# A graph-attention block on one Trainium2 core: turning the normalised rows on VectorE and through memory instead of on TensorE

## What is computed

```python
nx = _ln(x, ln1_g, ln1_b)
q, k, v = nx @ wq + bq, nx @ wk + bk, nx @ wv + bv        # split into 8 heads of 32
bias = where(adj > 0, 0.1 * adj * adj, -inf)
attn = softmax(q @ k.T / sqrt(32) + bias)
x1 = x + (attn @ v) @ wo + bo
n2 = _ln(x1, ln2_g, ln2_b)
out = x1 + gelu(n2 @ w1 + b1) @ w2 + b2                    # w1: 256 -> 1024, w2: 1024 -> 256
```

## Time and profile before

| | |
|---|---|
| median of three runs | 1406.34 us |
| the profiled execution | 1403.53 us, its span 1401.6 us |
| PE matmul busy | 1357.0 us, 97% of the span |
| DVE busy | 1188.8 us, 85% |
| ACT busy | 1135.6 us, 81% |
| POOL busy | 558.4 us, 40% |
| 16 DMA engines | 39.8% busy, 129 GB/s |
| mean granted clock of TensorE | 0.987 of full speed |

### The profile page before, as it was taken

How to read it: one execution, slowest core, us unless ns; L and a number is a source line. 1 busy time by engine, 2 the same in 40 slices (tenths; PEclk the granted TensorE clock), 3 DMA queues, 4 the chain that set the end, 5 groups by cost and what they waited for, 6 DMA issues and landing times.

```text
span 1401.6 us, 34084 instructions
## 1 busy us (share of the span) xinstructions
PE 1357.0 (97%) x11612; PEld 1167.6 (83%) x11612; DVE 1188.8 (85%) x2002; ACT 1135.6 (81%) x3336; POOL 558.4 (40%) x553
## 2 busy tenths in 40 slices
PE   8679999999999999999999999999999999999997
PEld 7568888888888888888888888888888888888876
DVE  4888898888898888898888889888889888889862
ACT  3678889888888888888988888988888888888753
POOL 3353334544333454333545333454333345433320
PEclk8789999999999999999999999999999999999999
DMA  4434333444333444333444433343443344433330
GB/s 150 132 125 143 130 117 122 154 134 144 127 117 125 139 142 142 120 127 121 137 149 131 135 130 118 122 153 127 145 132 110 126 146 142 142 120 121 103 116 23
DMA packets 147257, 180.17 MB, mean 129 GB/s; under 512 B 13584, under 2 KB 130576, under 8 KB 147216
## 3 DMA queue, kind: packets, MB, share of 16 engines
q1 hardware_dynamic: 147216, 179.63, 39.8%
HBM read 95.69 MB, written 83.89 MB: 128 GB/s over the span
## 4 chain that ended last, share of the span: by engine, by line
PE 91%; ACT 5%; DVE 2%; issue 1%; POOL 0%; DMA 0%; SPq 0%; ACTq 0%; DVEq 0%; POOLq 0%
PE work L378 27%; PE work L380 25%; PE work L379 25%; PE area L436 6%; PE work L483 4%; PE work L457 4%; ACT qk_all L656 2%; ACT soft L613 1%; DVE soft L842 0%; ACT late_memory L680 0%; ACT late_memory L691 0%; PE work L385 0%; DMA wa_raw<-in_L_gnn_wq 0%; DVE wa_raw L854 0%; DVE soft L818 0%
## 5 line engine op out<-in xcount | busy, mean ns | idle before, releaser
L613 ACT ACTIVATE soft<-soft,nmax 128x128 f32<-128x128 f32 x1024 | 396.9, 395 | 4.7 <-DVE nmax L826 4.4
L1018 POOL TENSOR_TENSOR ve<-mv,eps 128x4 f32<-128x4 f32 x64 | 13.0, 203 | 771.9 <-DVE mv L891 664.6
L378 PE MATMUL work<-w_hi,hid_parts 128*128 128x256 f32 x1024 | 295.4, 288 | 1.4 <-ACT late_memory L691 1.1
L380 PE MATMUL work<-w_hi,hid_parts 128*128 128x256 f32 x1024 | 286.0, 279 | 0.0
L379 PE MATMUL work<-w_lo,hid_parts 128*128 128x256 f32 x1024 | 285.9, 279 | 0.0
L927 DVE TENSOR_TENSOR hid_parts<-late_memory,hid_parts 128x512 fp32r<-128x512 f32 x256 | 225.2, 882 | 21.8 <-ACT hid_parts L701 21.6
L691 ACT ACTIVATE late_memory<-work,b_col 128x512 f32<-128x512 f32 x256 | 171.9, 683 | 69.6 <-PE work L380 53.3
L378 PE MATMUL work<-nt_hi,w_hi 128*128 128x512 f32 x512 | 211.8, 414 | 3.9 <-DVE nt_lo L917 3.9
L378 PEld LDWEIGHTS work<-w_hi,hid_parts 128*128 128x128 f32 x1024 | 191.9, 187 | 12.0 <-DVE xt_lo L917 5.8
L379 PE MATMUL work<-nt_lo,w_hi 128*128 128x512 f32 x512 | 201.4, 393 | 0.0
L380 PE MATMUL work<-nt_hi,w_lo 128*128 128x512 f32 x512 | 200.5, 392 | 0.0
(11 more groups left out here) (95 smaller groups left out, 3075.7 us busy)
## 6 DMA issues: line engine op xcount, KB each, us to landing
moved_blocks<-wa_raw SPq DMA_DIRECT2D x128, 512.0 KB, 2.7
probt<-moved_blocks SPq DMA_DIRECT2D x512, 128.0 KB, 2.9
xin<-in_x SPq DMA_DIRECT2D x32, 512.0 KB, 3.9
out<-res SPq DMA_DIRECT2D x128, 128.0 KB, 2.1
adj_in<-in_adj SPq DMA_DIRECT2D x32, 256.0 KB, 2.9
res<-in_L_gnn_w SPq DMA_DIRECT2D x1, 1024.0 KB, 9.9
late_memory<-in_L_gnn_w SPq DMA_DIRECT2D x1, 1024.0 KB, 12.4
wa_raw<-in_L_gnn_wq SPq DMA_DIRECT2D x1, 256.0 KB, 3.9
```

What stands on the lines that cost most here:

```text
L378: pe.matmul(o, lhs_hi, rhs_hi, start=first, stop=False)
L380: return pe.matmul(o, lhs_lo, rhs_hi, start=False, stop=last)
L613: a = act.activation(soft[:, b % 2, h, :], soft[:, b % 2, h, :], ACT.Exp, bias=nmax[:, b % 2, h:h + 1], accum_out=rsum[:, b % 2, h:h + 1])
```

## The change

Both turns leave TensorE. VectorE transposes the normalised rows of a whole group in 32x32 blocks into a buffer (`flat_blocks`, one instruction of 128x1024 for each kind). One DMA sends that buffer to DRAM (`send_flat`) and four bring it back (`fetch_flat`) over the old normalised rows (`xraw` is `xhat`'s memory, `nraw` is `nhat`'s). ScalarE makes the high part from there (`flip_hi`), and `flip_lo` moves from VectorE to GpSimd. `ident`, its build and the 16 matmuls against it at the start are gone.

The x rows are prepared one step sooner (normalised for group `step + 2`), and the MLP is later: the first two `up` units of a group still run in step 2, at its end, the others and `down` in step 3 (`-3`). In the diff the second `flip_lo` and the last `body` are GpSimd's; the bodies of the other engines are left out, and their new order is shown further down in three pieces. The bodies of all engines are in a new order, and so is `UNITS`, from 30 units to 26. Another waiting rule is added to `stats1`, and the small bias products of the start move by one score.

```diff
-AWAKE = 16
-UNITS = [("mix", 0, -1, 3), ("nt", 0, -2, 0), ("nt", 1, -2, 1), ("qk", 2, 0, 2), ("qk", 3, 0, 0),
+UNITS = [("v", 1, 0, 0), ("mix", 2, -1, 3), ("up", 2, -3, 1), ("up", 3, -3, 2), ("proj", 2, -1, 3),
...
-FIRST, EARLY, LATE = -2, 4, 2
+FIRST, EARLY, LATE = -2, 6, 2
...
+        flat = {k: sb(f"{k}_flat", [P, RPB, GB * DC, HD]) for k in ("xt", "nt")}
...
+        nraw = late_memory[:, 0:GB * D]
+        xraw = xhat[:, :, :].rearrange("p b d -> p (b d)")
...
+            def send_flat(step, off, kind):
...
+                sp.wait_ge(flat_ready[kind], step.through(off, 1, 0))
+                sp.dma_start(moved_flat[kind].rearrange("i k j n -> (i k) (j n)"),
+                             flat[kind][:, :, :, :].rearrange("p j m t -> p (j m t)")).then_inc(flat_sent[kind], 16)
+
+            def fetch_flat(step, off, kind):
...
+                raw = xraw if kind == "xt" else nraw
+                sp.wait_ge(flat_sent[kind], step.through(off, 1, 0, 16))
+                for j in range(RPB):
+                    sp.dma_start(raw[j * HD:(j + 1) * HD, :].rearrange("p (i n) -> p i n", i=RPB),
+                                 moved_flat[kind][:, :, j, :].rearrange("i k n -> k i n")).then_inc(flat_landed[kind], 16)
...
-            pe.wait_ge(ident_ready, 1)
-            for _ in range(AWAKE):
-                pe.matmul(spare, ident[:, :], ident[:, :], start=True, stop=True)
...
-            def flip(step, off, kind, c):
...
-                src, ready = (xhat, xhat_ready) if kind == "xt" else (nhat, nhat_ready)
-                free(step, kind, c)
-                for b in range(GB):
-                    if c == 0:
-                        pe.wait_ge(ready, step.through(off, GB, b))
-                    mm = pe.transpose(work[:, bank_of(kind, c), b * P:(b + 1) * P],
-                                      src[:, b, c * P:(c + 1) * P], ident[:, :])
-                mm.then_inc(full[kind], 1)
...
             def flip_hi(step, off, kind, c):
...
-                act.wait_ge(full[kind], step.through(off, DC, c))
-                act.activation(dst[:, c, :], work[:, bank_of(kind, c), :], ACT.Copy)\
-                   .then_inc(hi_taken[kind], 1)
+                act.wait_ge(flat_landed[kind], step.through(off, 1, 0, LAND))
+                act.activation(dst[:, c, :].rearrange("p (b i t) -> p b i t", b=GB, i=RPB),
+                               raw.rearrange("p (i b c t) -> p b i c t", i=RPB, b=GB, c=DC)[:, :, :, c, :],
+                               ACT.Copy).then_inc(hi_taken[kind], 1)
...
             def norm1(step, off, b):
...
-                    need(act, full["xt"], step.through(off - 1, DC, DC - 1))
+                    need(act, taken["xt"], step.through(off - 1, DC, DC - 1))
...
             def stats1(step, off):
...
+                need(dve, x_rstd, step.through(off - 1, 1, 0))
...
-            def flip_lo(step, off, kind, c):
...
-                dve.tensor_tensor(lo[:, c, :], work[:, bank_of(kind, c), :], hi[:, c, :].bitcast(F32),
-                                  ALU.subtract).then_inc(taken[kind], 1)
+            def flat_blocks(step, off, kind):
...
+                src, ready = (xhat, xhat_ready) if kind == "xt" else (nhat, nhat_ready)
+                need(dve, flat_sent[kind], step.through(off - 1, 1, 0, 16))
+                if kind == "nt":
+                    need(dve, taken["nt"], step.through(off - 1, DC, DC - 1))
+                dve.wait_ge(ready, step.through(off, GB, GB - 1))
+                dve.transpose(flat[kind][:, :, :, :], src.rearrange("p b d -> p (b d)")
+                              .rearrange("p (m j k) -> p j m k", j=RPB, k=HD)).then_inc(flat_ready[kind], 1)
...
+            def flip_lo(step, off, kind, c):
...
+                pool.wait_ge(hi_taken[kind], step.through(off, DC, c))
+                pool.tensor_tensor(lo[:, c, :].rearrange("p (b i t) -> p b i t", b=GB, i=RPB),
+                                   raw.rearrange("p (i b c t) -> p b i c t", i=RPB, b=GB, c=DC)[:, :, :, c, :],
+                                   hi[:, c, :].bitcast(F32).rearrange("p (b i t) -> p b i t", b=GB, i=RPB),
+                                   ALU.subtract).then_inc(taken[kind], 1)
...
             def body(step):
-                rstd_of_x(step, 1)
                 result_start(step, -2)
+                residual_start(step, 0)
+                flip_lo(step, 1, "xt", 0)
+                flip_lo(step, 1, "xt", 1)
+                rstd_of_x(step, 2)
                 rstd_of_n(step, -1)
-                residual_start(step, 0)
-                edges(step, 1)
+                flip_lo(step, -2, "nt", 0)
+                flip_lo(step, -2, "nt", 1)
+                edges(step, 2)
```

## The result

The kernel after takes 1410.72 us (median of 18 runs, 1403.65 to 1415.22), the one before 1406.25 us in the same comparison. The ratio is 1.0038, with a 95% interval of 1.0025 to 1.0050: slower by 0.4%, where I had forecast 1371 us and a range of 1354 to 1402. The profiled execution after has a span of 1412.7 us.

The account below looks back on a forecast made before the run. TensorE's work was taken to bound the steady part. -59.5 (PE) + 9 (waits) + 15.5 (added step) + 5 (first group) - 5 (end) = -35, from 1406.3 to 1371 us, range 1354 to 1402.

Parts of the forecast that it names:

- PE, per step: TensorE's steady step: transposes and a wait go, 0.20 us returns; 1.86 us less, floor 39.78 us, -59.5 us over 32 groups.
- What must fit under the floor: Steady step: DVE 36.8, ACT 37.9, POOL 22.6 us fit under 39.78; waits 0.3 us a step, +9 us (0 to +54).
- GpSimd's subtractions hold VectorE: Rival, steady step: four new subtractions add 5.2 us to DVE, 42.0 us a step, 1426 us; 0.13 shared with late turn.
- The turn that is late in each step: Rival, steady step: PE waits for xt_lo or nt_lo; 2 us late gives 1420, 1 us 1391; 0.13 shared with GpSimd's holds.
- ScalarE as the bound: Rival, steady step: ACT's 37.9 us plus remaining waits bound it; 1409, or 1385 with half; no chance of its own.
- its first version: ScalarE rival with 3.5 us of its waits remaining: step 41.4 us, total +2.4, 1409 us.
- The page on table loads: ScalarE rival's support: 1380 ns drain per table switch; two new switches 5.3 us, ACT needs 40.6 a step, 1385 us.
- The two ends: Filling and emptying the pipeline: added attention step +15.5 us, first group +5 us, end -5 us.
- The third step with attention alone: Start of pipeline: one more step of about 33 us with 17.5 us of PE work; +15.5 us idle.
- The end: Last group's turn, now covered by the MLP of group 30; -5 us (-8 to 0).
- The first group: Start: longer way to PE's first projection, +7.3 us, part made up behind it; +5 us taken (0 to +13).

Follow-up runs that it names:

- the kernel with 24 activations: 24 tiny unused activations added on ScalarE in written-out step 2, ahead of the loop, against the kernel after; 1388.65 us, ratio 0.9878 to the kernel before.
- the kernel with both repairs: Kernel after with all steps written out, late loads behind the first x return, small bias products one score later; 1368.96 us, ratio 0.9747 to the kernel before.

## Why the prediction was wrong

I go by its own steps. Written out, without the loop's stall, the kernel takes 1382 us, which lies in my range; with the start repaired as well it is 1369, about my forecast. The kernel as it is loses the gain to one thing that I never looked at, and to one that I sized too small.

**PE, per step: right.** The floor I had at 39.78 us, and a written-out step takes 39.88. Without the loop 28 groups take 1113.68 us and before 1161.90, 48.2 less, 1.72 each. My 1.86 less 0.3 is 1.56.

**What must fit under the floor: right in work, wrong in what it left out. This is the step that failed.** I took +9 us for all waits, "what PE had before for all causes". It is about +3 in written-out steps and 33 with the loop: 11 x 2.75 = 30 us more. My loads were right: ScalarE has 1049.38 / 28 = 37.5 us of work a step (37.9 in the text), the turns on VectorE take 1.24 and 1.22. But I added up busy times and followed waits on semaphores only; the jump back had no term in the sum, because in the kernel before it cost nothing, 0.24 us from the jump to the next instruction. In the kernel after ScalarE's code lies so that each of the 11 jumps is followed by a fetch and stops it for 3.9 to 4.6 us. I had counted instructions for their durations and never for their number and place: 8 more for the loop's body on ScalarE (280 from jump to jump and not 272), and some 265 more ahead of it. That ScalarE now has little room makes the stall dear, 2.25 us a time and not 0.56, but doesn't cause it.

The rows of the groups for the kernel after, which answer to the earlier trace rows:

```profile
L934 DVE TENSOR_TENSOR hid_parts<-late_memory,hid_parts 128x512 fp32r<-128x512 f32 x256 | 228.6, 921 | 27.4 <-ACT hid_parts L706 26.8
L1040 POOL TENSOR_TENSOR xt_lo<-xhat,xt_hi 128x512 fp32r<-128x512 f32 x64 | 117.4, 1847 | 56.1 <-ACT xt_hi L650 56.1
L1040 POOL TENSOR_TENSOR nt_lo<-late_memory,nt_hi 128x512 fp32r<-128x512 f32 x64 | 81.0, 1287 | 5.8 <-ACT nt_hi L650 5.8
L696 ACT ACT_TABLE_LOAD x59 | 75.7, 1283 | 6.0 <-PE work L404 5.0
L617 ACT ACT_TABLE_LOAD x58 | 74.4, 1283 | 1.1
L926 DVE STREAM_TRANSPOSE xt_flat<-xhat 128x1024 f32<-128x1024 f32 x32 | 39.6, 1237 | 0.8 <-ACT xhat L674 0.7
```

**The rivals.** GpSimd's subtractions hold VectorE: falls. `hidden_lo` has a mean of 921 ns against 882, 10 us in 256; one of the two pairs of new subtractions is held itself, the x rows at 1847 ns, the n rows at 1287 as I took them. The turn that is late in each step: falls, PE waits for `xt_lo` in the steady part nowhere, and its 24.4 us are three waits of the start. ScalarE as the bound: the nearest, since the time came out as its first version says (1409). But its reason, the order's waits that would stay, is not what happened. In the written-out kernel ScalarE still waits 2.3 us a step ((1113.68 - 1049.38) / 28) and the step is 39.88 all the same; what makes the long steps is the stall. The page on table loads (the Trainium skill, ScalarE: Activation LUTs, What ACT_TABLE_LOAD costs) with its further 1380 ns at each switch is not borne out: 117 loads with 7.1 us of idle time ahead of them all, and ScalarE's written-out step fits into 39.88 us, for which 40.6 would have been too much.

**The two ends.** The third step with attention alone takes 33.3 us, forecast 33. PE's idle time from the mix of group 0 to that of group 3 went from 14.1 to 35.9 us, +21.8 where I had +15.5: besides the added step, the low parts of the late weights fell under POOL's additions. VectorE and POOL of the kernel after:

```profile
84.52 5.28 DVE L786 SCALAR_TENSOR_TENSOR w_lo<-res,cols_in,w_hi 128x1024 fp32r<-128x1024 f32 x2 [1.07 <-ACT w_hi L609]
89.72 3.34 DVE L789 TENSOR_TENSOR w_lo<-late_memory,w_hi 128x2048 fp32r<-128x2048 f32 x1
```

```profile
85.39 3.33 POOL L1060 TENSOR_TENSOR x<-xin,bo_rows 128x1024 f32<-128x1024 f32 x1
88.91 5.26 POOL L1040 TENSOR_TENSOR xt_lo<-xhat,xt_hi 128x512 fp32r<-128x512 f32 x2 [0.19 <-ACT xt_hi L650]
```

The first pair took 2.48 us before; both engines are slowed here, and PE waits 11.3 us behind it. The end: PE's idle time fell from 9.8 to 2.9 us, -6.9 for my -5.

**The first group: the second term that was too small,** +5 us with a bound of 13, measured +19.6 to the mix of group 0. Of these 9.2 - 2.9 = 6.3 are the way out behind the loads, which I had seen as possible and not put into the sum. That the bias products move by one score stands in the description of the change, and I gave it no price. With both repaired the mark is at 54.41, +4.7. A part is chance: up to that mark the kernel with 24 activations has the same work as the kernel after and reached it at 63.87, with a clock of 0.86 and not 0.74 between first projection and mix; the kernel with both repairs had 0.84 there.

## What to carry to other kernels

A change that adds, removes or moves instructions can make a loop's jump back dear on one engine, though the order, the waits and the busy times are all right. It shows as idle time with no releaser at the loop's first instruction, as a late first instruction behind the jump, and as packets on the instruction queue in the middle of the loop, where the kernel without a stall has none. How much of it reaches the end depends on that engine's slack. Compare the steps inside a loop with those written out, one by one: a period of two in steps that should be equal can be the loop. Before a loop is made longer or shorter, count each engine's instructions in it and ahead of it, and write it out once to see what it costs.

## What was not expected of the hardware

- A loop's jump back cost ScalarE 2.5 to 3.2 us of idle time, or nothing, depending on where the code lay: moved by 24 instructions it vanished, moved by 8 it stayed, 4 instructions fewer a loop (8 fewer ahead) removed it, and 14 more ahead brought it back.
- With twice the code an iteration PE stalled twice (2.46 and 3.10 us), VectorE once (2.88): 7.9 us a jump ((1153.16 - 1113.68) / 5), nearly three times the cost of the short loop, a part of it by TensorE's clock, at 0.50 for 6.8 us behind the jumps.
- POOL's subtraction on the returned x rows and VectorE's instructions with two operands in SBUF slow each other: 1847 ns where the same form, beside VectorE's additions from PSUM, takes 1287. 52 of the 64 run beside a `hidden_lo`, and 27 of these beside the scaling of the probabilities as well; those 27 take 2.10 us on average, the other 25 take 1.64.

What stays open: how long a block is, and whether the kernel before can be given the stall. Its loop of 272 instructions doesn't stall where it lies; a few dozen tiny activations ahead of it, tried one number after the other, would tell, and that was not run.
